# Attention scores of a four-stage network: larger plain units, smaller turned units, triangles zeroed after the exponential

## What is computed

```python
x = L0_attn_z                                     # (4, 512, 128)
x = x + _L0_attn_ref(_layernorm(x), ...)          # 16 heads of 8, causal
x = x + _L0_ffn_ref(_layernorm(x), ...)           # 8 experts, 2 of them a row
x = x + _L1_attn_ref(_layernorm(x), ...)          # 16 heads of 8, one K and V, rotary, causal
x = x + _L1_ffn_ref(_layernorm(x), ...)           # 4-bit quantised, gated

attn = jnp.einsum('nhqd,nhkd->nhqk', q, k) * scale
attn = jnp.where(causal, attn, -jnp.inf)
attn = jax.nn.softmax(attn, axis=-1)
out = jnp.einsum('nhqk,nhkd->nhqd', attn, v)
```

## Time and profile before

| | us |
|---|---|
| median of 3 runs | 744.9 (743.86 to 745.43) |
| the profiled execution | 745.5 |
| its span in the trace | 743.8 |
| round 0 of layer 0, plain scores alone | 35 to 79 |
| rounds 1 to 3 of layer 0 | 79 to 237 |
| turned scores alone, routing | 237 to 289 |
| experts | 291 to 461 |
| rounds 1 to 3 of layer 1 | 488 to 638 |
| turned scores alone with the quantised stage's first steps | 638 to 677 |
| the rest of the quantised stage | 677 to 744 |

### The profile page before, as it was taken

One profiled execution on the slowest core, in us unless ns is written; L12 is line 12 of the kernel. 1 busy time (PEld: TensorE's weight loads), 2 busy tenths in 40 slices (PEclk: granted clock), 3 DMA queues, 4 the chain that ended last, 5 costly groups with the idle time before them and its releaser, 6 DMA issues.

```text
span 743.8 us, 12641 instructions
## 1 busy us (share of the span) xinstructions
PE 598.1 (80%) x4398; PEld 392.5 (53%) x4398; DVE 500.8 (67%) x1344; ACT 315.2 (42%) x478; POOL 213.7 (29%) x216
## 2 busy tenths in 40 slices
PE   1478788998779657998898798869799899998564
PEld 0233455565545423877796576335455555566344
DVE  6578767686776662675453574876776778666993
ACT  1111355665435524443453333046356465674221
POOL 5312010011103313354053412363022010345764
PEclk9995699999979969999998999579899999999985
DMA  7405477466631203122131311422012111000000
GB/s 239 129 23 149 102 155 215 78 160 134 140 58 38 59 5 103 31 71 71 41 89 36 111 30 34 115 52 66 24 46 67 45 25 36 24 12 1 15 14 29
DMA packets 50590, 53.43 MB, mean 72 GB/s; under 512 B 6271, under 2 KB 43377, under 8 KB 50497
## 3 DMA queue, kind: packets, MB, share of 16 engines
q1 hardware_dynamic: 48481, 48.42, 26.0%
q0 software_dynamic: 2048, 4.20, 2.1%
HBM read 33.56 MB, written 21.10 MB: 73 GB/s over the span
## 4 chain that ended last, share of the span: by engine, by line
PE 55%; DVE 31%; issue 7%; POOL 3%; ACT 2%; DMA 1%; SPq 0%; POOLq 0%; DVEq 0%; ACTq 0%
PE ps L583 10%; PE ps L538 8%; DVE mx L764 7%; PE ps L562 6%; PE ps L1179 5%; PE ps L609 4%; DVE xn L1074 3%; PE ps L541 3%; PE ps L1167 2%; PE ps L591 1%; PE ps L1158 1%; DVE stats L1064 1%; PE ps L566 1%; PE ps L1161 1%; PE ps L1159 1%
## 5 line engine op out<-in xcount | busy, mean ns | idle before, releaser
L764 DVE TENSOR_REDUCE mx<-ps 128x1 f32<-128x384 f32 (+3 forms) x352 | 215.7, 637 | 81.3 <-PE ps L541 79.4
L658 ACT ACTIVATE pT<-ps 128x1024 f32<-128x1024 f32 x160 | 161.9, 1022 | 106.9 <-PE ps L566 89.0
L541 PE MATMUL ps<-mask_qk,identb 128*128 128x128 bf16 (+2 forms) x352 | 95.5, 271 | 0.0
L538 PE MATMUL ps<-stA 96*128 96x128 bf16 (+3 forms) x256 | 72.3, 345 | 28.7 <-DVE mx L764 23.8
L538 PE MATMUL ps<-kA,stA 96*128 96x128 bf16 (+3 forms) x256 | 69.2, 328 | 24.7 <-DVE mx L764 18.3
L583 PE MATMUL ps<-pT,vA 128*32 128x512 f32 (+3 forms) x1024 | 80.5, 450 | 0.7 <-ACT pT L658 0.7
L583 PEld LDWEIGHTS ps<-pT,vA 128*32 128x32 f32 x1024 | 40.5, 113 | 34.4 <-issue 24.4
L538 PEld LDWEIGHTS ps<-stA 96*128 96x128 bf16 x256 | 22.5, 105 | 60.5 <-DVE mx L764 41.7
L1206 ACT ACTIVATE pT<-ps 128x512 f32<-128x512 f32 x46 | 27.4, 595 | 60.8 <-PE ps L1161 60.8
L1179 PE MATMUL ps<-w_sb,pT 128*128 x368 | 51.0, 284 | 1.7 <-ACT pT L1216 1.7
L562 PE MATMUL ps<-stB 96*128 96x512 bf16 (+3 forms) x256 | 50.9, 312 | 1.1 <-ACT pT L658 0.9
(11 more groups left out here) (297 smaller groups left out, 1183.0 us busy)
## 6 DMA issues: line engine op xcount, KB each, us to landing
stA<-stack_scratch SPq DMA_DIRECT2D x48, 192.0 KB, 3.4
stB<-stack_scratch SPq DMA_DIRECT2D x48, 192.0 KB, 4.6
stack_scratch<-part SPq DMA_DIRECT2D x12, 384.0 KB, 3.0
stack_scratch<-part SPq DMA_DIRECT2D x12, 256.0 KB, 3.3
...
```

The lines of the kernel that those rows point to most:

```text
L538: pe.matmul(ps[:, bank, m * w:(m + 1) * w], stA[:, 0, h, qb * P:w], kk[:, 0:w], start=(m == 0), stop=False)
L541: pe.matmul(diagonal, identb[:], mask_qk[:].unsqueeze(1).broadcast_to([P, len(heads), P]), start=False, stop=True).then_inc(a["sc"], 1)
L658: act.activation(dst_, src, ACT.Exp, scale=SCALE).then_inc(a["ex"], 1)
L764: nc.vector.tensor_reduce(mx[:, g % 2, qb, heads[0]:heads[0] + nh], ps[:, S_BANK[n % 2], 0:nh * w].rearrange("p (h k) -> p h k", h=nh), AX ...
```

## The change

**Plain scores.** Six units a group: two heads of query block 3, the other two, the same for block 2, four heads of block 1, four of block 0. They go to two pairs of banks, (0, 1) and (2, 3), in turn. A unit has up to 1,024 columns and one reduction, over both banks. The mask matmul stands at the end of each bank; their number stays 11. In layer 1 the first twelve units (ALONE) and the next one use pair (0, 1) alone, each waiting for the reduction before, since the experts' H still uses banks 2 and 3.

**Turned scores.** Ten units a group in single banks, 4 and 5 in turn: two a head (key block 0; blocks 1 and 3) and two of two heads each (block 2). The mask matmuls and mask_kq are gone. ACT writes 512 powers an instruction, and POOL then sets the triangle of each diagonal block to zero (affine_select, one or two blocks of 128x128 a unit) and counts it on a new semaphore (below). PV waits for ten of those instead of for the powers.

**Order.** MP stands first in a group, and S0, ST0, S1, ST1 stand ahead of MT and PV; the rest alternates as the diff says. The steps of other stages keep their places in the misc lists.

```diff
--- before.py
+++ after.py
@@ -64,19 +64,23 @@
-S_BANK = (0, 1)
-ST_BANK = (2, 4)
+S_BANK = (0, 2)
+ST_BANK = (4, 5)
...
-S_UNITS = [(0, (0, 1, 2, 3)), (1, (0, 1)), (1, (2, 3))] + [(2, (j,)) for j in range(HG)] + [
-    (3, (j,)) for j in range(HG)]
+S_UNITS = [(3, (0, 1)), (3, (2, 3)), (2, (0, 1)), (2, (2, 3)), (1, (0, 1, 2, 3)), (0, (0, 1, 2, 3))]
...
-NV = HG + 1
+NV = 2 * HG + HG // 2
...
+ALONE = 2 * NS
@@ -104,14 +108,19 @@
-            for v in range(NV + 1):
-                if s < B:
-                    o.append(("S", s, g, 2 * v))
-                if v < NV and 1 <= s <= B:
-                    o.append(("ST", s - 1, g, v))
-                if v < NV and s < B:
-                    o.append(("S", s, g, 2 * v + 1))
-                o += [(n, b, k, 0) for n, b, k in misc[v] if 0 <= b < B]
...
+            o += between(0) + scores(0) + turned_scores(0) + scores(1) + turned_scores(1) + between(1)
+            o += turned_scores(2) + scores(2) + between(2) + turned_scores(3, 4) + scores(3) + between(3)
+            o += turned_scores(5) + scores(4) + turned_scores(6) + between(4)
+            o += turned_scores(7) + scores(5) + turned_scores(8) + between(5) + turned_scores(9)
@@ -517,6 +526,10 @@
+        def score_pair(layer, n):
+
+            return S_BANK[0 if layer and n <= ALONE else n % 2]
...
+                alone = layer and n <= ALONE
+                if alone and n:
+                    pe.wait_ge(a["maxd"], n)
+                elif layer and n == ALONE + 1:
+                    pe.wait_ge(M["ge"], HALVES * NTL)
+                elif n >= 2:
                     pe.wait_ge(a["maxd"], n - 1)
...
-
-                if u < HG:
-                    pe.matmul(ps[:, base, 0:P], identb[:], mask_kq[:], start=False, stop=True)
-                    last = pe.matmul(ps[:, base + 1, :].rearrange("p (a c) -> p a c", a=NB)[:, 0:4:3, :], identb[:],
-                                     mask_kq[:].unsqueeze(1).broadcast_to([P, 2, P]), start=False, stop=True)
-                else:
-                    for c in range(2):
-                        last = pe.matmul(ps[:, base + c, :].rearrange("p (h k) -> p h k", h=2)[:, :, 0:P], identb[:],
-                                         mask_kq[:].unsqueeze(1).broadcast_to([P, 2, P]), start=False, stop=True)
+                    last = pe.matmul(bank[:, at:at + w], kk[:, kb * P:(kb + 1) * P], stB[:, 0, h, kb * P:T],
+                                     start=(at == 0), stop=(at + w == 512))
                 last.then_inc(a["st"], 1)
             elif name == "PV":
-                pe.wait_ge(a["ex"], (i + 1) * NV)
+                pe.wait_ge(below, (layer * B * G + i + 1) * NV)
...
-                nc.vector.tensor_reduce(
-                    mx[:, g % 2, qb, heads[0]:heads[0] + nh],
-                    ps[:, S_BANK[n % 2], 0:nh * w].rearrange("p (h k) -> p h k", h=nh), AX.X, ALU.max,
-                ).then_inc(a["maxd"], 1)
...
+                nc.vector.tensor_reduce(mx[:, g % 2, qb, heads[0]:heads[0] + nh], src, AX.X, ALU.max).then_inc(a["maxd"], 1)
...
+            elif name == "ST":
+
+                n = i * NV + u
+                pool.wait_ge(a["ex"], n + 1)
+                row = powers(g, u)
+                blocks = row[:, :, 0:P] if u >= 2 * HG else diagonal_blocks(row, u)
+                nc.gpsimd.affine_select(blocks, blocks, compare_op=ALU.is_ge, fill=0.0, base=0,
+                                        pattern=[[0, blocks.shape[1]], [1, P]], channel_multiplier=-1).then_inc(below, 1)
...
-                bank = ps[:, ST_BANK[0] + n % 2, :]
+                bank = ps[:, S_BANK[1] + n % 2, :]
```

More of the change, by code:

```diff
@@ L469, in network @@
             A.append({n: sem(f"{n}_{layer}") for n in both + rotary * layer})
+        below = sem("below")
         loads = {n: [sem(f"{n}{g}") for g in range(G)] for n in ("loadA", "loadB", "mload")}
@@ L549, in attention_tensor @@
                 if n == 0 and layer:
-                    for read in ("ge", "hT", "yb", "xsplit"):
+                    for read in ("hT", "yb", "xsplit"):
                         pe.wait_ge(M[read], HALVES * NTL)
@@ L1210, in experts_scalar @@
                     act.wait_ge(M["y"], n - 1)
[L1211 removed]
+                act.activation(hT[:, n % 2, :], ps[:, ST_BANK[0], :], ACT.Copy).then_inc(M["hT"], 1)
             elif name == "Y":
@@ L1666, in _ @@
             nc.gpsimd.tensor_copy(identb[:], ident[:]).then_inc(made, 1)
-            for m, step, mul in ((mask_qk, -1, 1), (mask_kq, 1, -1)):
+            for m, step, mul in ((mask_qk, -1, 1),):
                 link(nc.gpsimd, nc.gpsimd.memset(m[:], 0.0))
```

89 lines of the change are left out of this document (52 added, 37 removed).

## The result

| | us |
|---|---|
| median before, beside it | 744.38 (4 runs) |
| median after | 754.03 (752.17 to 755.11, 4 runs) |
| ratio | 1.013, interval 1.010 to 1.016 |
| forecast | 723 (703 to 742) |
| the profiled execution of after, its span | 754.92, 752.7 |

The account below looks back on a forecast made before the run. The prediction took PE to bound the kernel, with 0.97 us idle a group. From 745.5 us it took 29.2 (mixed groups) and 5.0 (plain scores alone), added 8 and 4 for POOL's queue, and forecast 723 us, range 703 to 742.

Parts of the forecast that it names:

- What bounds the kernel: Undisturbed layer-0 groups: PE is the bound, busy 10.73 of 11.70 us, with 0.97 us idle a group.
- The split of that term: Groups with plain and turned scores: 0.97 us idle plus 0.90 of masks less 0.60 of stalls, 1.27 us gained each.
- PV hidden with 0.15 to spare: In each group the last select ends at 1.65 us and PV is due at 1.8, so its wait is hidden.
- Two places where the new queue costs: POOL's queue: scatters before the experts end 8 us later; selects behind layer 1's late quantising step cost 4 us.
- Rival B: Turned units in single banks: PE stalls for ACT 1.4 us a group rather than 0.6; 740 us, chance 0.20.
- Rival C: POOL's selects gate every PV, slower from a mean select of about 0.75 us; about 800 us, chance 0.07.
- Rival D: DVE's port lock with POOL holds MP's four operations back, 1.0 us a group beyond slack; 747 us, chance 0.06.
- Turned-only groups, nothing left: Layer 1's eight turned-only groups: mask time saved (8 x 0.9) is offset by ten powers in two single banks.
- Plain scores alone: Plain-only groups: larger units remove half of DVE's idle time, 3.6 us in layer 0 and 1.4 in layer 1.
- Layer 1's ten mixed groups: Layer 1's groups with plain and turned scores together: 1.27 us gained a group, 12.7 us over the ten.
- Experts: Expert stretch: no change; layer 1's first two plain groups sharing one bank pair there cost 0, bounds +-2 us.

Follow-up runs that it names:

- masks_back: The changed kernel with the turned masks on PE again and no selects; units, banks and order as changed: 728.8 us, ratio 0.979.
- no_triangles: masks_back without the turned masks, so neither selects nor masks and the unwanted triangles stay: 725.6 us, ratio 0.976.
- wait_only: masks_back, with GpSimd waiting at each turned unit for its power but doing nothing: 736.7 us, ratio 0.989.
- work_only: wait_only plus a select of the same size on a tile nobody uses; PV waits for the powers alone: 750.2 us, ratio 1.007.
- deep: masks_back with four single banks instead of two for the turned units of each layer's last sequence: 727.6 us, ratio 0.977.
- deep_late: deep with MT and PV behind four of the ten turned units in the turned-only groups: 720.3 us, ratio 0.969.
- hybrid: masks_back with selects instead of masks except in layer 0's sequences 2 and 3 and layer 1's sequence 3: 735.8 us, ratio 0.987.
- experiment 4: The changed kernel with selects only away from routing and tail, mask matmuls on PE in the other groups: 735.8 us, ratio 0.987.
- fill_routing: masks_back with selects only in layer 0's sequences 2 and 3, plus 40 idle PE matmuls in layer 0's turned-only groups: 747.7 us.

## Why the prediction was wrong, point by point

- **What bounds the kernel** held where the forecast looked: the calm groups went from 11.69 to 10.47 us. PE's 0.97 us of idle time a group was there to be had.
- **The split of that term** was wrong. It put 0.90 us to the masks and 0.37 to the waits. masks_back shows 0.90 for units, banks and order, where PE is busy 73.37 of 75.51 us; the masks' removal brings 0.32, or 0.44 without selects (no_triangles), since PE's other waits come next (1.7 us over seven groups, 4.8 without the masks). Over the whole kernel it is worth 3 us, not 18 to 29.
- **PV hidden with 0.15 to spare** held in the calm groups: no wait on a select there.
- **The failed step** is "Two places where the new queue costs". The rule by which the prediction found them, what stands behind a select in POOL's queue and who waits for it, was right, and both places are real: the gather stretch is 4.3 us longer than before, 5 longer than in masks_back, forecast 8; layer 1's last five are 4.4 us longer than in masks_back, with 4.2 us of PE's waits for selects, forecast 4. But it was applied to two steps out of many. The routing powers, the scatters of the first rounds and the rotary sum of layer 1 stand in the same queue; for the routing groups the forecast wrote a gain of 0.8 us each, for the others no cost. It measured +15 us in the routing groups and +4.3 at L1's start, both against masks_back. Selects were priced as work beside PV (3.5 us of a free 9), while each of them is also a wait for ACT, and neither the waits (7 us, wait_only) nor the work (11 us more, work_only) was charged to the steps behind.
- **Rival B**, PE waiting for ACT: such waits come to 1.9 us in the seven calm groups, 0.27 a group, for 0.5 in the forecast and 1.4 in the rival.
- **Rival C**, GpSimd as the gate, had the right engine and the wrong mechanism: a select's mean is 0.375 us, far under its 0.75 (by its own sum the sign turns at 0.64), and the kernel is slower all the same. Most of the loss, 21 of 25 us, is there when no PV waits for GpSimd (work_only), and for that no rival stood.
- **Rival D**, the lock, is small where the prediction looked for it. The MP operation of line 798 takes 338 ns in the mean with selects about and 233 in no_triangles. All four together are 5.3 us longer over 32 groups, 0.17 a group and not 1.0. The groups of that line (busy, mean ns | idle before) in after, then in no_triangles:

```profile
L798 DVE TENSOR_SCALAR mpart<-mx 128x16 bf16<-128x16 f32 x32 | 10.8, 338 | 0.7
```

```profile
L798 DVE TENSOR_SCALAR mpart<-mx 128x16 bf16<-128x16 f32 x32 | 7.5, 233 | 0.7
```

  The Trainium skill, "SBUF — State Buffer", section "Who interferes with whom", says that the ports which DVE shares with GpSimd are an exclusive lock for a whole instruction. The trace agrees in kind. The prediction didn't ask the same of the routing steps, where DVE's instructions take 3.2 us more in work_only than in wait_only; how much of that PE waits for is open.
- **Turned-only groups, nothing left**: wrong by 5.9 us in layer 1 (masks_back). Two single banks cost 3.1, MT and PV behind half as many columns 2.3 (deep, deep_late).
- **Plain scores alone**: under-sized. Start is 11.0 us shorter, forecast 3.6. From MP to MP, a plain group takes 7.6 and 8.2 us in after, 10.3 and 9.5 before; the forecast counted DVE's idle time only, half of it.
- **Layer 1's ten mixed groups**: -6.4 for -12.7. The last five gained 8.5 us, nearly what the forecast gave to seven; the first five lost 2, in masks_back too (69.8 us for 68.05). The rotary sum isn't the reason: ACT waits for it 7.7 us there, 9.2 before. What is new is that PE waits for ACT's powers, 5.2 us in three waits (5.8 in the changed kernel), where before it has no such wait. No run separated this.
- **Experts** +3.7, over the bounds of 2 given for the shared pair: this stretch varies between 156.6 and 160.3 us among the experiments. Between masks_back and hybrid 2.7 of 3.0 us go with a lower granted clock in two tiles (experiment 4); for the changed kernel it is open.

## What to carry to other kernels

Moving an operation to an engine with free time also puts its wait into that engine's queue. Before costing such a move, list every other step of that engine in the stretch, and ask for each how late it gets if it must wait until the new operand is there, and who stands behind it. Relieving the busiest engine can give back much less than the work taken off it (here 0.32 us a group for 0.9), because the next wait is close behind: run the change without the thing moved (here masks left where they were) to see which part earns.

## What was new about the chip

A wait costs as a place in the order even with no work behind it: eight scatters sat 8.67 us behind waits for powers that they don't use, and the kernel was 8 us longer (wait_only). More work for PE can raise the granted clock without any gain in time: 11 us fewer at 1.2 GHz in fill_routing, 747.7 us for 747.3. In another place a lower clock went with lost time: the same 47 matmuls of two expert tiles kept PE busy 7.9 us in a stretch of 10.7 at a clock of 1.00 (masks_back), and 10.5 us in one of 13.4 at 0.74 (hybrid). A select of 128x128 took 0.29 us and of two blocks 0.41 in undisturbed places, and 0.82 in one of the routing rounds (the longest of all took 0.87):

```profile
230.52 0.82 POOL L834 TENSOR_SCALAR_AFFINE_SELECT pT<-pT 128x256 f32<-128x256 f32 x1 [3.98 <-ACT pT L677]
101.19 0.41 POOL L834 TENSOR_SCALAR_AFFINE_SELECT pT<-pT 128x256 f32<-128x256 f32 x1 [0.20 <-ACT pT L677]
```
